# Separate places for the probability products in the step order of a two-layer attention, expert and FFN kernel

## What is computed

```
x = x + attn0(layernorm(x))    # softmax over keys with 0 <= q - k <= 127
x = x + experts(layernorm(x))  # top 2 of 8, each silu(a) * b in 512 columns, then 512 to 256
x = x + attn1(layernorm(x))    # softmax over keys k <= q, biases on q, k, v and out
x = x + layernorm(x) @ (ternary(weight) * scale).T
```

## Time and profile before

| what | value |
|---|---|
| median of 3 runs | 2713.08 us (2712.34 to 2715.16) |
| profiled execution, its own time | 2714.14 us |
| profiled execution, span | 2712.2 us |
| mean granted TensorE clock | 0.947 of full |
| busy share of the span | PE 89%, PEld 61%, DVE 65%, ACT 50%, POOL 33% |
| a0 | 0 to about 910 us |
| experts | about 950 to 1585 us |
| a1 | about 1590 us to the end |

### The profile page before, as it was taken

One profiled execution on the slowest core, in us unless ns is written; L12 is line 12 of the kernel. 1 busy time (PEld: TensorE's weight loads), 2 busy tenths in 40 slices (PEclk: granted clock), 3 DMA queues, 4 the chain that ended last, 5 costly groups with the idle time before them and its releaser, 6 DMA issues. The chain is left out here.

```text
span 2712.2 us, 50761 instructions
## 1 busy us (share of the span) xinstructions
PE 2406.1 (89%) x17551; PEld 1655.8 (61%) x17722; DVE 1752.9 (65%) x5775; ACT 1354.6 (50%) x2419; POOL 900.5 (33%) x847
## 2 busy tenths in 40 slices
PE   4899999999999489999999946898999999999996
PEld 2465566556665379889888833455555555555553
DVE  4777877887786454444454426777777777777761
ACT  2465666656665233333333312465566665665564
POOL 1446545654652300000000033444444444444300
PEclk8899999999999789999999966899999999999998
DMA  4676776677643577877787634455444444454420
GB/s 149 196 221 209 226 213 213 215 226 224 199 151 101 200 259 274 287 276 280 262 285 247 236 123 139 142 151 144 126 133 126 125 126 129 139 147 127 132 56 16
DMA packets 259616, 490.19 MB, mean 181 GB/s; under 512 B 25608, under 2 KB 191112, under 8 KB 249416
## 3 DMA queue, kind: packets, MB, share of 16 engines
q1 hardware_dynamic: 241944, 435.23, 51.2%
q0 software_dynamic: 17456, 52.19, 5.7%
HBM read 299.65 MB, written 186.52 MB: 179 GB/s over the span
## 5 line engine op out<-in xcount | busy, mean ns | idle before, releaser
L900 ACT ACTIVATE a_pr<-a_bank 128x512 f32<-128x512 f32 (+1 forms) x1152 | 637.4, 574 | 387.0 <-PE a_bank L1323 254.6
L1184 DVE CUSTOM_DVE_ANT_0 a_junk<-a_bank,a_smask 128x256 bf16<-128x256 f32 (+3 forms) x1536 | 651.5, 463 | 131.8 <-PE a_bank L1420 126.7
L1464 PE MATMUL a_bank<-a_pr,a_va 128*32 128x256 f32 (+3 forms) x4096 | 349.2, 417 | 22.0 <-ACT a_pr L900 14.4
L1781 PE MATMUL e_bank<-e_xh,e_under 128*128 128x512 f32 (+1 forms) x1248 | 361.4, 375 | 1.4 <-DVE e_xl L1757 1.4
L1420 PE MATMUL a_bank<-a_kst,a_qst 96*128 96x128 bf16 (+3 forms) x1024 | 266.0, 314 | 30.7 <-DVE a_nmax L1184 12.8
L1323 PE MATMUL a_bank<-a_mask,a_identb 128*128 128x128 bf16 (+2 forms) x981 | 279.8, 285 | 0.0
L1446 PE MATMUL a_bank<-a_qst,a_kst 98*128 98x512 bf16 (+3 forms) x1024 | 253.8, 305 | 12.2 <-ACT a_pr L900 10.7
L1781 PEld LDWEIGHTS e_bank<-e_xh,e_under 128*128 128x128 f32 x1248 | 222.2, 189 | 40.7 <-DVE e_xl L1757 1.8
L1781 PE MATMUL e_bank<-e_xl,e_under 128*128 128x512 f32 (+1 forms) x624 | 233.1, 374 | 0.0
L1668 POOL DMA_DIRECT2D results_dram<-e_yt x39 | 29.3, 753 | 612.6 <-DVE e_yt L1736 595.1
L1691 ACT ACTIVATE e_sa<-e_bank,e_b 128x512 f32<-128x512 f32 (+1 forms) x156 | 101.5, 651 | 247.3 <-PE e_bank L1781 225.6
(11 more groups left out here) (214 smaller groups left out, 5004.9 us busy)
## 6 DMA issues: line engine op xcount, KB each, us to landing
e_under<-ws_dram SPq DMA_DIRECT2D x39, 2048.0 KB, 9.0
a_parts_dram<-a_parts SPq DMA_DIRECT2D x224, 256.0 KB, 3.1
e_under<-ws_dram SPq DMA_DIRECT2D x39, 1024.0 KB, 6.0
e_under<-a_parts_dram SPq DMA_DIRECT2D x96, 384.0 KB, 6.7
a_kst<-a_parts_dram SPq DMA_DIRECT2D x96, 384.0 KB, 9.8
...
```

The costliest lines, as they stand in the source:

```text
L900: nc.scalar.activation(pr[b][:, h:h + per, :], TB_[at % 2][:, 0:per * w].rearrange("p (h w) -> p h w", h=per), ACT.Exp, scale=scale).then_ ...
L1184: last = nc.vector.tensor_tensor_reduce(junk[:, at % 2, j * w:(j + 1) * w], SB_[at % 2][:, j * w:(j + 1) * w], smask[:, T - w:T], scale=-1 ...
L1464: last = nc.tensor.matmul(PVB[32 * j:32 * (j + 1), q0:q0 + w], va[i % 2][:, b, (g * HG + j) * VW:(g * HG + j) * VW + 32], pr[b][:, j, :], ...
L1781: last = nc.tensor.matmul(out[:, 0:s.columns], first(s.slot, low)[:, kc, col:col + P], x[s.slot][:, kc, 0:s.columns], start=(p == 0), stop ...
```

## The change

`PV(g,b)` gets a name of its own, `PV<g><b>`, in `PLACES` and `EDGES`; `main<g>` now holds the T steps alone. And every number of `PLACES`, `EDGES` and `LAGS` of both a0 and a1 is new. No instruction is added or removed and none has another size, and the experts' part is as it was; only the order on each engine differs. The tables are 34 lines longer, so that L1007 of before is L1041 after, and so on for all lines of the rows here.

```diff
 PLACES = {
     "a0": {
...
-        "turn2": (0.4488, 0.00273), "score": (0.6608, 0.00246), "exp2": (0.6953, 0.01414), "place": (0.7844, 0.00273),
...
+        "turn2": (0.4958, 0.00398), "score": (0.7667, 0.15576), "exp2": (0.7866, 0.07318), "place": (0.8283, 0.0002),
...
     "a1": {
-        "vcopy": (0.0217, 0.00253), "minus0": (0.684, 0.0136), "load": (0.6906, 0.00166), "aggr": (1.0437, 0.23537),
-        "gather0": (0.2768, 0.00026), "mix0": (0.7995, 0.03408), "gather1": (0.9319, 0.00199), "mix1": (0.95, 0.01241),
...
+        "v": (0.008, 0.0008), "vcopy": (0.0954, 0.00063), "minus0": (0.7748, 0.03564), "load": (0.6389, 0.00126),
+        "aggr": (1.0371, 0.0004), "gather0": (0.4267, 0.00158), "mix0": (0.7368, 0.02826), "gather1": (0.8093, 0.0053),
+        "mix1": (1.0113, 0.00077), "stats": (1.0124, 0.00742), "shift": (0.373, 0.00842), "norm": (0.0994, 0.00649),
...
                 for g, steps in enumerate(main_steps(i)):
                     for k, step in steps:
-                        put(i, "main" + str(g), step, k)
+                        put(i, "main" + str(g) if step[0] == "T" else "PV" + str(g) + str(step[3]), step, k)
```

More of the change, by code:

```diff
@@ L137 @@
[L137 to L140, removed]
[8 rows of a table added]
+        "minus1": (0.1997, 0.01356), "back": (-0.0022, 0.02752), "out": (0.1578, 0.00048), "add": (0.1895, 0.00293),
@@ L141 @@
+        "vcopy": (0.0004, 0.0034), "minus0": (0.6265, 0.0282), "load": (0.5567, 0.00517), "aggr": (0.5592, 0.00361),
+        "stats": (0.7065, 0.00016), "norm": (0.0887, 0.00591), "turn": (0.2145, 0.00014), "stack": (0.8814, 0.00414),
[5 rows of a table added]
     },
     "a1": {
[8 rows of a table removed]
-        "minus1": (0.1158, 0.06305), "back": (0.08, 0.00566), "out": (0.13, 0.0072), "add": (0.1262, 0.00613),
-        "stats2": (0.1994, 0.00694), "aggr2": (0.2785, 0.00232), "norm2": (0.2747, 0.01033), "y": (0.3071, 0.02303),
-        "turn2": (0.3648, 0.00979), "last": (0.4473, 0.00021), "final": (0.4285, 0.01229), "v": (0.024, 0.04954),
@@ L158 @@
+        "turn": (0.1603, 0.00663), "stack": (1.0918, 0.00799), "bias": (-0.7708, 0.00305), "quantise": (0.3999, 0.00153),
[4 rows of a table added]
     },
@@ L203 @@
+            "sums0": (0.1313, 0.00264), "sums1": (0.4646, 0.00716), "sums2": (0.7687, 0.00015), "sums3": (0.9483, 0.01062),
+            "turn2": (0.5484, 0.00089), "v": (0.2321, 0.25692), "vcopy": (0.238, 0.00553), "y": (0.0193, 0.00753),
         },
         15: {
[5 rows of a table removed]
[L210 to L211 removed]
@@ L212 @@
-            "sums3": (1.0763, 0.01296), "turn2": (0.4941, 0.00683), "y": (0.3169, 0.02491),
[9 rows of a table added]
+            "scale3": (-0.0088, 0.01961), "scatter": (0.1139, 0.00055), "score": (0.5718, 0.0024), "spots": (0.7162, 0.00301),
+            "stats2": (0.1785, 0.00612), "sums0": (0.1467, 0.00548), "sums1": (0.4878, 0.01799), "sums2": (0.7791, 0.00066),
+            "sums3": (0.8312, 0.00458), "turn2": (0.4886, 0.00155), "y": (0.2899, 0.00026),
         },
         16: {
-            "aggr2": (0.2414, 0.01348), "back": (0.092, 0.00997), "exp2": (0.8619, 0.01974), "flip3": (-0.1491, 0.01027),
@@ L216 @@
-            "gates": (0.5719, 0.00557), "norm2": (0.2405, 0.00361), "pads": (-0.3637, 0.01151), "scale3": (0.1594, 0.00104),
-            "scatter": (0.6182, 0.01096), "score": (0.6254, 0.00901), "spots": (1.1048, 0.00947), "stats2": (0.2537, 0.006),
-            "turn2": (0.5346, 0.02141), "y": (0.1423, 0.03986),
+            "add": (0.2141, 0.02057), "aggr2": (0.6156, 0.00885), "back": (-0.0191, 0.03101), "exp2": (0.7948, 0.09757),
+            "flip3": (-0.1415, 0.00037), "gates": (0.7365, 0.0002), "norm2": (0.2823, 0.05193), "out": (0.2816, 0.00141),
@@ L219 @@
+            "pads": (-0.0527, 0.00335), "place": (0.9731, 0.0127), "scale3": (-0.0415, 0.08007), "scatter": (0.7782, 0.00974),
+            "score": (0.7526, 0.15576), "spots": (0.8903, 0.00115), "turn2": (0.5816, 0.00699), "y": (0.2528, 0.00103),
         },
         17: {
-            "scatter": (-0.1414, 0.03602),
+            "scatter": (0.1528, 0.00024),
         },
@@ L286 @@
         "DVE": {
-            "S": 0.0446, "turn": 0.0698, "minus": -0.0078, "aggr2": 0.0647, "aggr": 0.0579, "rope": -0.0071, "part": 0.1199,
+            "S": 0.0243, "turn": 0.0223, "minus": -0.0414, "aggr2": 0.0643, "aggr": 0.423, "rope": -0.0421, "part": 0.1468,
         },
         "SP": {
-            "minus": -0.0244,
+            "minus": 0.0383,
         },
         "ACT": {
-            "back": -0.0049, "turn2": 0.0138, "turn": -0.0452, "part": 0.0419, "T": -0.0055, "minus": -0.0061,
+            "back": 0.0141, "turn2": 0.0561, "turn": -0.0018, "part": 0.0932, "T": 0.0239, "minus": 0.0198,
         },
         "POOL": {
-            "aggr": 0.0025, "rope": -0.0031, "aggr2": -0.1282, "part": 0.066,
+            "aggr": 0.3301, "rope": -0.2551, "aggr2": -0.2067, "part": -0.1258,
         },
@@ L300 @@
         "DVE": {
-            "rope": -0.0001, "minus": -0.0627, "bias": -0.2088, "quantise": -0.1579, "part": -0.0681, "S": 0.0088,
-            "aggr2": -0.0442, "aggr": 0.0343, "turn": 0.0224,
+            "rope": 0.0164, "minus": -0.0775, "bias": 0.06, "quantise": 0.0522, "part": 0.1986, "S": 0.0102, "aggr2": -0.0048,
+            "aggr": 0.008, "turn": 0.0214,
         },
         "POOL": {
-            "aggr2": 0.0061, "aggr": 0.0645, "part": 0.0964, "rope": 0.1237,
+            "aggr2": 0.1822, "aggr": 0.1343, "part": 0.1325, "rope": 0.1403,
         },
         "ACT": {
-            "turn": 0.01, "part": -0.0174, "back": -0.0097, "turn2": 0.0004, "minus": 0.0211, "T": 0.0013,
+            "turn": -0.0013, "part": 0.0065, "back": 0.0071, "turn2": 0.0087, "minus": 0.0253, "T": 0.0017,
         },
         "SP": {
-            "minus": 0.0534,
+            "minus": 0.2103,
         },
```

40 lines of the change are left out of this document (16 added, 24 removed), and 200 rows, old and new, of tables (EDGES, PLACES).

## The result

The changed kernel takes 2627.15 us (median of 4 runs, 2623.91 to 2636.06) where the kernel before takes 2713.35. The ratio is 0.9687 with a 95% interval of 0.9662 to 0.9712: 3.1% faster, 86 us.

What follows compares the result with a forecast made beforehand. PE was taken to bound the kernel, with only its 55 us of standing still per stretch open to the change. The terms summed to -35.9 us, 2678.2 for the profiled execution, forecast 2677 us, range 2650 to 2712.

Steps and rivals of the forecast that it cites:

- term 1: a1: choice 1's gathers get more time before DVE needs them, so PE's wait at back mostly goes: -34.0 us.
- Term 2: a1: earlier mixes push DVE's maxima, so PE's scores wait 0.4 us more in 15 sequences: +6 us, bounds 0 and 15.
- Term 3: a1's head: aggr moves ahead of a waiting mix, so PE's first transposition lies beside the mixes: -2.7 us, bound -6.5.
- Terms 4 and 6: a0: turn2 no longer waits for the rope, -13.6 us; the last PV waits less for its exponential, -3.6 us.
- terms 5 and 7: a0: project(1) directly behind project(0) waits for banks, +4.5 us; POOL's eight scatters ahead of aggr2 delay norm2, +7.5 us.
- Gathers as late as now: a1 rival: stores load the same DMA engines, so gathers land late again; term 1 is -26, time 2685 us; chance 0.13.
- Late stack loads: a1 rival: minus and the loads behind it come later, 35 us that take back term 1, time 2712 us; chance 0.08.
- POOL's chain: a0 rival: later stack loads, then scatters and aggr2, cost 4.3 us in 14 sequences, 60 us, time 2730; chance 0.11.
- term 7: a0: all eight scatters ahead of aggr2 on POOL make norm2 later; the chain just fits PE's work: +7.5 us.
- Better: Rival: costs 2, 5 and 7 don't come and 10 us of a0's remaining waits go: 2649 us; chance 0.10.

Runs made afterwards that it cites:

- e3: Kernel before, with only the four mixes of choice 0 in a1 about 5 us earlier on DVE, so choice 1's gathers precede the stack loads: 2657.7 us, ratio 0.9799.
- e12: The same kernel as e11, run again beside e13: 2570.8 us, ratio 0.9481.
- e13: Changed kernel with a0's second scale ahead of the split and SP's write ahead of the store, without e11's step in a1: 2588.1 us, ratio 0.9541.
- e8: e3's kernel with, at a1's head, DVE's aggregation of the first sequence ahead of the next one's first mix: 2652.5 us, ratio 0.9782.
- e2: Kernel before with only a0's new numbers and PV places, a1 in the old order: 2723.6 us, ratio 1.0049.
- e4: Changed kernel with a0's split of the first half's maxima 5 us earlier on DVE in every sequence but the first: 2607.4 us, ratio 0.9618.
- e5: Changed kernel with a0's second scale ahead of the maxima's split on DVE, the transposition one pair of scores later on PE: 2601.3 us, ratio 0.960.
- e10: Changed kernel with one ACT cast of part later in a0 from the second sequence, so POOL's instruction misses DVE's split: 2602.1 us, ratio 0.9605.
- e11: e13's kernel with a1's split of the first half's maxima one maximum earlier on DVE from the third sequence: 2670.0 us, ratio 0.9701.
- e7: Changed kernel with the products with the probabilities back at main's places in a1's sequences 1 to 12: 2680.7 us, ratio 0.9883.

## Why the prediction was wrong

**The step that failed** is term 1: "I take 36.6 us off and leave 0.2 us in each of 13 sequences", and ahead of it the premise that the change "can only act on the 55 us that PE stands still in either stretch". The mechanism was right: the gathers of choice 1 go out ahead of the stack loads, land in 2.8 us at the median, and PE's wait is gone. But the wait was priced at its own length. e3 shows that the gather alone gives 54.5 us, one and a half times PE's wait, since TensorE ran at half clock behind ten of thirteen such waits. PE's busy time, which was to stay within 1%, fell in a sequence of a1 from about 58.9 to 55.9 us, 5%, and in a0 it rose by as much. The windows by sequence (0.95 to 1.00) were there to be read; the forecast read the waits and took the mean clock of 0.97 in a1 for a given.

**Term 2** (+6, bounds 0 to 15) had the right sign: the scores now wait 15.6 us for maxima in a1 where it was 5.5. The reason given, the order's balance, was not the main one: e12 against e13 shows that one cast waiting for POOL makes all of it, 17 us, a little over the upper bound. **Term 3** (-2.7, bound -6.5) was too small for what it priced: PE's first transposition comes 7.2 us earlier in e8 and 7.1 in the change. What that is worth in the end is not clear of the noise (4.6 us in e8). It was priced as if the mixes still stood in the way, and they are short; what stood in the way was the 6.46 us of the earlier trace rows. Behind it the next three sequences of the head gained another 9.9 us and the tail 7.9, by the profiles. No experiment took these apart.

**a0** was forecast at -5 and cost 11 (e2). Terms 4 and 6 came true: neither `turn2` nor the products wait any more. The costs of terms 5 and 7 did not come: PE has no wait of `project(1)`, and none that leads to POOL's scatters. ACT does wait longer for POOL's L797 ahead of `norm2`, 26.0 us where it was 10.8 over 100 to 850 us, but no wait of PE stands behind it. What came was on no list: the transposition of the maxima waits 27.5 us and takes the clock from 0.99 to 0.92. e4, e5 and e10 show its cause from three sides. The prediction asked what POOL's queue makes late, not what a POOL instruction does to DVE beside it. It could be read before. These are DVE rows of the kernel before, in a0:

```profile
543.82 0.83 DVE L1194 CAST a_nparts<-a_nmax 128x32 bf16<-128x32 f32 x1
...
546.30 1.65 DVE L1038 TENSOR_TENSOR a_bs<-a_sc,a_bnb 128x32 f32<-128x32 f32 x1
```

and POOL's of the same stretch:

```profile
542.48 2.13 POOL L804 TENSOR_TENSOR a_qk<-a_qk,a_parts 128x1024 f32<-128x1024 f32 x1
545.77 2.13 POOL L808 TENSOR_TENSOR a_parts<-a_qk,a_parts 128x1024 bf16<-128x1024 f32 x1 [1.16 <-ACT a_parts L875]
```

The addition L1038 takes 1.03 to 1.67 us in the 13 sequences between 100 and 850 us; in the changed kernel, where no POOL instruction lies beside it, the same one (L1072) takes 0.19 in all 13. This one ends at 547.95, POOL's at 547.90. The cast (0.83) ends at 544.65, POOL's at 544.61.

The Trainium skill has the rule, which the forecast missed: page "SBUF — State Buffer", section "SBUF: two separate sides", says that VectorE and GpSimd share one pair of SBUF ports as an exclusive lock, held for the whole instruction, for which a VectorE operation with two SBUF inputs (against a GpSimd one that reads SBUF) or in a two-port mode has to wait while GpSimd works. The traces agree, in both stages: in the changed kernel's trace all 29 casts and all 16 subtractions of the split that begin well inside an elementwise instruction of POOL's last until 0.04 to 0.05 us behind its end. They also show what is left standing. The maxima, ropes and scales, which read PSUM, ran beside the same POOL instructions at their usual length (0.42 us for a maximum of 256 columns, 0.68 for a rope). And so did the layernorm's statistics (L1019), which read one tile in SBUF, none of 36 held up:

```profile
390.67 1.40 DVE L1019 BATCH_NORM_STATS2 a_stats<-a_xt 128x6 f32<-128x256 f32 x4
```

```profile
389.86 2.12 POOL L842 TENSOR_TENSOR a_parts<-a_qk,a_parts 128x1024 bf16<-128x1024 f32 x1 [1.16 <-ACT a_parts L909]
```

So theory A of e11, any DVE instruction with all its data in SBUF, is too wide: the casts and those with two inputs in SBUF are the ones that wait.

**The rivals.** *Gathers as late as now* (0.13) fell: the longest landing is 6.4 us (the forecast's own sign was under 6, missed by little) and DVE no longer waits for `a_yg`. The rule on the queues' turns that the prediction takes from the Trainium skill spoke for this rival and the rows for the forecast, and the rows were right. *Late stack loads* (0.08) and *POOL's chain* (0.11) don't show in PE's waits, but e10 shows the latter's first link, POOL waiting for the stacks, once a cast comes some 3 us later. The price of the latter, 60 us, does not follow from its rows: no row shows the typical landing from which its 2.7 us are counted (the median of the earlier trace rows is 7.7, not 9.8), and it sets the chain of 39.1 us against 34.8 of work where term 7 took 37.5; by the latter it is 1.6 us in each of 14 sequences, 22. *Better* (0.10, 2649) was nearest, and still 22 us short.

**Of the balance** of a1's steady part, 5.6 us for each sequence, e3 gives 4.7. The remaining 0.9 is PE's busy time at full clock, 57.3 against 55.9 us, less about 0.6 of new idle time. It needs the products' own places as the other numbers stand (e7), but which of their neighbours makes matmuls denser wasn't tried.
